# Layer 2's two blocks of a four-layer decoder: where the norms of batch 0 and batch 1 are made

## The reference, cut to what matters

```python
x = x + _L1_attn_ref(_layernorm(x, axis=-1), ...)
...
def _mha(x, y, ...):
    xn = _ln(x, lnx_g, lnx_b)
    yn = _ln(y, lny_g, lny_b)
    ...                       # 16 heads of 32, softmax of all scores, in block 1 masked after it
    x_out = x + o @ li1_w + li1_b
    h = jax.nn.gelu(_ln(x_out, ln3_g, ln3_b) @ li2_w + li2_b, approximate=False)
    return x_out + h @ li3_w + li3_b
x = _ln(xx, ln1_g, ln1_b)
x = x + _mha(x, x, ..., causal=True)
x = _ln(x, ln2_g, ln2_b)
return x + _mha(x, ee, ..., causal=False)
```

## Time and profile before

| | us |
|---|---|
| median of 3 runs | 2310.19 (2309.71 to 2314.41) |
| the profiled execution, its own time | 2309.87 |
| its span, first to last instruction | 2308.1 |

### The profile page before, as it was taken

One profiled execution on the slowest core, in us unless ns is written; L12 is line 12 of the kernel. 1 busy time (PEld: TensorE's weight loads), 2 busy tenths in 40 slices (PEclk: granted clock), 3 DMA queues, 4 the chain that ended last, 5 costly groups with the idle time before them and its releaser, 6 DMA issues.

```text
span 2308.1 us, 57670 instructions
## 1 busy us (share of the span) xinstructions
PE 2019.8 (88%) x22720; PEld 1471.6 (64%) x22720; DVE 1353.8 (59%) x3602; ACT 896.5 (39%) x3421; POOL 561.4 (24%) x1358
## 2 busy tenths in 40 slices
PE   8999999989977898998977887999999999789744
PEld 4899998877566565567855654666554545556522
DVE  6667666755255787545635624787263220678797
ACT  2455554543155564212334422665110111256511
POOL 3566664222011000102425512331000000401111
PEclk9555555999989899899988988999999999889956
DMA  3000002004000001100030000000030000000000
GB/s 136 4 5 5 5 5 79 1 1 182 0 5 2 14 12 53 86 0 24 1 133 2 1 1 7 9 11 2 1 151 0 1 0 4 1 15 12 2 0 16
DMA packets 8027, 57.21 MB, mean 25 GB/s; under 512 B 793, under 2 KB 5249, under 8 KB 5985
## 3 DMA queue, kind: packets, MB, share of 16 engines
q1 hardware_dynamic: 7760, 53.54, 6.1%
HBM read 52.62 MB, written 0.92 MB: 23 GB/s over the span
## 4 chain that ended last, share of the span: by engine, by line
PE 67%; DVE 12%; issue 9%; ACT 6%; POOL 5%; DMA 1%; POOLq 0%; DVEq 0%; SPq 0%; ACTq 0%
PE banks L265 43%; PE banks L270 8%; PE banks L1364 7%; PE banks L937 3%; ACT memory L985 2%; PE banks L963 2%; DVE memory L1466 2%; PE banks L1517 1%; DVE memory L1247 1%; ACT memory L1391 1%; DVE memory L824 1%; POOL memory L1423 1%; ACT memory L1398 1%; DVE memory L1472 1%; DVE memory L1475 1%
## 5 line engine op out<-in xcount | busy, mean ns | idle before, releaser
L265 PE MATMUL banks<-memory 128*112 128x256 f32 (+7 forms) x4192 | 1129.8, 425 | 65.9 <-POOL memory L2077 8.0
L265 PEld LDWEIGHTS banks<-memory 128*128 128x128 f32 (+3 forms) x4192 | 704.8, 195 | 396.4 <-issue 250.9
L270 PE MATMUL banks<-memory 112*125 112x112 f32 (+3 forms) x2000 | 305.9, 286 | 108.6 <-DVE memory L824 54.9
L270 PEld LDWEIGHTS banks<-memory 112*125 112x125 f32 (+3 forms) x2000 | 238.6, 172 | 224.6 <-issue 114.6
L1364 PE MATMUL banks<-memory 128*128 128x8 bf16 (+2 forms) x10752 | 308.1, 174 | 13.7 <-DVE memory L1449 1.4
L1364 PEld LDWEIGHTS banks<-memory 128*128 128x128 bf16 x10752 | 296.7, 104 | 25.7 <-POOL memory L1423 21.5
L985 ACT ACTIVATE memory<-banks,memory 112x375 f32<-112x375 f32 x384 | 215.4, 579 | 25.5 <-DVE memory L1023 25.1
L1023 DVE TENSOR_REDUCE memory<-banks 112x2 f32<-112x750 f32 x192 | 171.1, 934 | 37.1 <-PE banks L937 36.9
L1466 DVE TENSOR_REDUCE memory<-banks 128x48 f32<-128x192 f32 x448 | 122.1, 291 | 62.6 <-PE banks L1364 47.9
L840 POOL TENSOR_TENSOR memory<-memory 112x1 f32<-112x1 f32 x71 | 39.2, 552 | 355.7 <-DVE memory L819 354.3
L1031 DVE COPY memory<-banks 125x448 f32<-125x448 f32 x192 | 117.0, 620 | 10.5 <-PE banks L270 6.1
(11 more groups left out here) (234 smaller groups left out, 2425.2 us busy)
## 6 DMA issues: line engine op xcount, KB each, us to landing
memory<-in_l2x SPq DMA_DIRECT2D x1, 7680.0 KB, 21.6
memory<-in_l2f SPq DMA_DIRECT2D x1, 7168.0 KB, 20.1
memory<-in_l1f SPq DMA_DIRECT2D x1, 4617.0 KB, 14.8
memory<-in_ctxT SPq DMA_DIRECT2D x24, 187.5 KB
memory<-in_l2f SPq DMA_DIRECT2D x1, 4096.0 KB, 12.6
memory<-in_l3f SPq DMA_DIRECT2D x1, 3073.0 KB, 22.4
memory<-in_l2a SPq DMA_DIRECT2D x1, 3072.0 KB, 18.2
memory<-in_l0f SPq DMA_DIRECT2D x1, 2304.0 KB, 9.1
```

The costliest lines, as they stand in the source:

```text
L265: ins = self.nc.tensor.matmul(out, weights[i], acts[i], start=i == 0, stop=i == n - 1)
L270: return self.nc.tensor.transpose(out, in_, self.ident[0:n, 0:n])
```

## The change

Three things. First, batch 0's two norms of each block are made in the stage before the block: in layer 2's attention for block 1, by a new step `ahead` at the end of rounds 6, 7, 10 and 11 (statistics; then power, row, gain and shift on GpSimd; statistics of that; then power and row), and in the feed-forward between the blocks for block 2, with VectorE's parts after the adds of batch 3 and of batch 5. The base lies in `k.ahead`, the normalised row in a new buffer `k.ahead2`; the row is now made by GpSimd, which used to be VectorE's. The blocks' `prologue` loses `ln`, `stats` and `xn` of batch 0, and of `xm` only the copy with the bias stays. Second, in block 1 both norms of batch 1 go from `second` into `prologue`: statistics of the first ahead of everything, `xm` before the key projection, the second norm behind the query. Third, in layer 1's attention the statistics and the norm of batch 1 go from `second` into `prologue` too. In block 2 batch 1's norms stay in `second`. No DMA is added, moved or removed.

```diff
+        self.ahead2 = whole.take(D, parts=S)
...
+def ahead_block_dve(k, src, second):
+
+    if second:
+        k.nc.vector.wait_ge(*k.s.ahead_ready(1))
+    norm_row_stats(k, 0, k.ahead_stats, k.s.ahead_stat, k.ahead if second else src)
+
+
+def ahead_block_pool(k, src, rows, ln):
+
+    s, G = k.s, k.nc.gpsimd
+    norm_row(k, 0, k.ahead_stats, s.ahead_stat(1), s.ahead_rstd, k.ahead, src).then_inc(*s.gstep.up())
+    for n, op in ((ln, ALU.mult), (ln + 1, ALU.add)):
+        G.wait_ge(*s.gstep.now())
+        ins = G.tensor_tensor(k.ahead, k.ahead, rows[0:S, n, :], op)
+        ins.then_inc(*(s.gstep.up() if n == ln else s.ahead_ready.up()))
+
+
+def ahead_block_rows(k):
+
+    norm_row(k, 0, k.ahead_stats, k.s.ahead_stat(2), k.s.ahead_rstd, k.ahead2, k.ahead).then_inc(*k.s.ahead_ready.up())
...
-                xn = k.ahead if b < self.ahead else self.xn
+                xn = self.xn if b >= self.ahead else k.ahead2 if isinstance(self, L2Block) else k.ahead
...
-    prologue = (("xT", 0), ("parity", 0), ("k", 0), ("q", 0))
-    second = (("v", 0, 0), ("stats", 0, 1), ("xn", 0, 1), ("xT", 0, 1))
+    prologue = (("xT", 0), ("parity", 0), ("stats", 0, 1), ("k", 0), ("q", 0), ("xn", 0, 1))
+    second = (("v", 0, 0), ("xT", 0, 1))
...
+            if n in (6, 7, 10, 11):
+                yield "ahead", 0, (6, 7, 10, 11).index(n)
...
+        elif step == "ahead":
+            if i == 0:
+                V.wait_ge(*s.y_read(1))
+                ahead_block_dve(k, k.x[:, 0, :], False)
+            elif i == 2:
+                ahead_block_dve(k, k.x[:, 0, :], True)
...
-        if step == "stats":
+        if step == "ahead" and i == 3:
+            ahead_block_rows(k)
+        elif step == "ahead" and i == 1:
+            G.wait_ge(*k.landed["l2x_rows"].now())
+            G.wait_ge(*s.xT_full(1))
+            ahead_block_pool(k, k.x[:, 0, :], k.packs["l2x_rows"]["rows"], 0)
...
+    ahead = 1
...
-        return self.xms[b % 3]
+        return self.xms[b % 3] if b else self.k.ahead
...
-        elif step == "xm":
+        elif step == "xm" and b:
...
-            G.wait_ge(*s.xl_ready(b + 1))
-            G.tensor_tensor(xm, xm, self.row(self.ln), ALU.mult).then_inc(*s.gstep.up())
-            G.wait_ge(*s.gstep.now())
-            G.tensor_tensor(xm, xm, self.row(self.ln + 1), ALU.add).then_inc(*s.xm_ready.up())
-            G.wait_ge(*s.xm_ready(b + 1))
+            if b:
+                G.wait_ge(*s.xl_ready(b))
+                G.tensor_tensor(xm, xm, self.row(self.ln), ALU.mult).then_inc(*s.gstep.up())
+                G.wait_ge(*s.gstep.now())
+                G.tensor_tensor(xm, xm, self.row(self.ln + 1), ALU.add).then_inc(*s.xm_ready.up())
+                G.wait_ge(*s.xm_ready(b))
...
-    prologue = (("ln", 0), ("xm", 0), ("stats", 0), ("xn", 0), ("xT", 0), ("k", 0), ("q", 0))
-    second = (("v", 0, 0), ("ln", 0, 1), ("xm", 0, 1), ("stats", 0, 1), ("xn", 0, 1), ("xT", 0, 1))
+    prologue = (("ln", 0, 1), ("xT", 0), ("xm", 0), ("xm", 0, 1), ("k", 0), ("q", 0), ("stats", 0, 1), ("xn", 0, 1))
+    second = (("v", 0, 0), ("xT", 0, 1))
...
-    prologue = (("ln", 0), ("xm", 0), ("cstat", 0), ("stats", 0), ("cn", 0), ("xn", 0), ("xT", 0), ("q", 0), ("cT", 0),
-                ("k", 0), ("k", 1))
+    prologue = (("cstat", 0), ("cn", 0), ("xm", 0), ("xT", 0), ("q", 0), ("cT", 0), ("k", 0), ("k", 1))
...
+        else:
+            ahead_block_pool(self.k, self.into[:, 0, :], self.k.packs["l2x_rows"]["rows"], 2)
+            ahead_block_rows(self.k)
...
+            if not self.last and b in (HALF - 1, HALF + 1):
+                V.wait_ge(*s.x_ready(1))
+                ahead_block_dve(k, self.into[:, 0, :], b > HALF)
```

More of the change, by code:

```diff
@@ L1149, in order @@
     def order(self):
-        for kind, i in self.prologue:
-            yield kind, 0, i
+        for kind, i, *of in self.prologue:
+            yield kind, of[0] if of else 0, i
         yield "all", 0, 0
@@ L3221, in four_bit_rows, with norm_row_stats @@
         "p (i k n) -> p i k n", i=2, k=KD)
-def norm_row_stats(k, b, st, signal):
+def norm_row_stats(k, b, st, signal, src=None):
     s, V = k.s, k.nc.vector
-    V.bn_stats(st[:, 0:6], k.x[:, b, :]).then_inc(*s.vstep.up())
+    V.bn_stats(st[:, 0:6], k.x[:, b, :] if src is None else src).then_inc(*s.vstep.up())
     V.wait_ge(*s.vstep.now())
@@ L3232, in norm_row_stats, with norm_row @@
     V.tensor_scalar(st[:, 8:9], st[:, 7:8], EPS, None, ALU.add).then_inc(*signal.up())
-def norm_row(k, b, st, after, signal, into=None):
+def norm_row(k, b, st, after, signal, into=None, src=None):
     G = k.nc.gpsimd
@@ L3241, in norm_row @@
     into = k.row_norms[:, b, :] if into is None else into
[L3242 removed]
+    return G.tensor_scalar(into, k.x[:, b, :] if src is None else src, st[:, 6:7], st[:, 9:10], ALU.subtract, ALU.mult)
 def four_bit_values(k, values, y, sc):
```

2 lines of the change are left out of this document (1 added, 1 removed).

## The result

| | before | after |
|---|---|---|
| median of the runs compared, us | 2310.01 (2309.71 to 2314.41) | 2288.05 (2284.37 to 2290.48) |
| the profiled execution, its own time | 2309.87 | 2285.73 |
| its span | 2308.1 | 2283.9 |

The account below looks back on a forecast made before the run. TensorE, busy 88% of the span, was held to lose time only where it stands waiting for row norms or runs at half clock. Gains 3.1 + 12.6 + 5.0 = 20.7 us gave 2289.5 us, range 2283.5 to 2297.

Parts of the forecast that it names:

- Block 1, first wait: Block 1's head: without batch 0's norms on the path, the first row maximum comes 6.0 or 4.6 us earlier.
- Block 1, second wait: Batch 1's norm in block 1: its wait goes, ScalarE's value copy is late next, key projection gains 7.1 us.
- The rival, that another wait takes its place at the old time: Block 1: masks or exponentials hold TensorE's queue, the 7.1 us don't come; 13.6 instead of 20.7 us, 2296.6; chance 0.10.
- its counter-argument: Block 1: a mask is wanted only by its own four heads' transposes, said to stand behind the key projection.
- Block 1 together: Both waits of block 1 summed: 13.1 or 11.7 us gained, 12.6 taken.
- Layer 1's attention: Batch 1's norm wait goes, ScalarE's biased key copy is late next: neighbour matmuls 3.1 us earlier, between 1.8 and 3.53.
- Block 2: Block 2's head without batch 0's statistics and norms: query projection 5.3 us earlier; 5.0 us taken, between 3.8 and 6.5.
- up to 1.5 us are given back: Block 2's key matmuls: if the clock is still low there, up to 1.5 us of the gain is lost.
- What is added: Added statistics and norm steps in layer 2's attention and the feed-forward lie in idle time: nothing, bounds 0 and 1 us.
- The rival that ends slower than before: Late round of layer 2's attention: VectorE's wait for GpSimd's row delays the last output adds; 2315 if 26 us late; chance 0.02.
- The two clock cases: Clock low at all three heads and the keys: 2292.9, chance 0.13; clock stays high: 2283.7, chance 0.08.
- the prediction's slow case: Block 1's head: the 32 projections run mostly at half clock as before and take 5.38 us, against 4.1 at full.

Follow-up runs that it names:

- norm earlier: Changed kernel with batch 1's second norm in block 1 placed on VectorE ahead of the query instead of behind it; 2287.18 us, 0.9903 of before.
- both edits: Changed kernel with VectorE copying batch 0's values in block 1 and batch 1's second norm ahead of the query; 2282.14 us, 0.9872 of before.
- after, third: The changed kernel itself, unaltered, measured and profiled a third time; 2287.37 us, 0.9895 of before.
- Batch 0 only: Kernel before, with only batch 0's norms for block 1 made ahead in layer 2's attention; 2301.64 us, 0.9964 of before.
- value by VectorE: Changed kernel with batch 0's values in block 1 copied by VectorE instead of ScalarE; 2285.9 us, 0.9893 of before.

## Why the prediction held

**Block 1, first wait.** Right in its order, and in its bounds to 0.7 us. Projections were to start 2.6 us after the last add (1193.4 against 1190.84) and started 2.40 after it; they were to take 4.1 or 5.4 us and took 3.83 or 5.45; the maximum was to gain 6.0 or 4.6 and gained 6.7 (8.62 against 15.30) or 5.05. What was mis-sized: 0.16 us at the start of the projections, 0.27 in their full length, and batch 1's second norm ahead of the maximum, put at 0.8 us. It costs 0.56: "norm earlier" gives just that back at full clock (8.62 to 8.06), and "both edits" against "after, third" does at the slow one (10.25 to 9.69). "Batch 0 only", which has neither of batch 1's norms there, had its maximum 0.95 us earlier than the changed kernel at full clock; the other 0.39 are the first statistics ahead of the scaling (projections at 2.01 instead of 2.40).

**Block 1, second wait.** 7.1 us forecast, 7.04 measured (13.80 to 6.76), with the cause named beforehand and shown by "value by VectorE", which takes it away. The distance stood at 6.75 to 6.78 us in five profiles whatever the clock did. The rival, that another wait takes its place at the old time, is refuted by that. But its counter-argument was wrong in one step: the transposes that want the first mask stand ahead of the key projection, not behind it, and do wait for the mask (1.75 us, until 1197.76). It costs nothing because ScalarE's copy, at 1201.16, ends later still. The new wait of 2.94 us is the one that was forecast.

**Block 1 together.** 12.6 forecast; 11.1, 13.3 and 11.3 in three profiles, mean 11.9. The spread is the clock's, as the two bounds 11.7 and 13.1 had it, and slightly wider, because the loop behind adds its own. The assumption that an earlier head shifts all of its stage holds to 1.1 us here: the three profiles are 12.1, 13.7 and 12.1 us ahead at batch 1's key projection and 11.0, 13.3 and 11.3 at the block's end.

**Layer 1's attention.** 3.1 us forecast at the neighbour matmuls, 3.22 measured (15.05 to 11.83), bound by ScalarE's biased key copy as forecast. The statistics and the norm in the prologue cost the first maximum nothing. The whole layer gained 3.8 us on the mean of three profiles (411.02 to 407.23). In the first profile the attention's loop gave most of the gain back (107.70 us for the whole stage, before 108.65), and the unchanged stages behind it were 3.95 us shorter than before; in the other two the attention took 103.85 and 105.08, and the stages behind it were as long as before, to 0.3 us. The prediction had no term for such an exchange.

**Block 2.** 5.0 us taken, between 3.8 and 6.5; measured 6.5, 3.4 and 6.6 against the kernel before, 5.2 on the mean against 214.83. The query projection's gain was 6.16 us instead of 5.3: VectorE opened the stage 0.30 us after its release instead of 0.65, and the last of the context statistics, 0.48 us before, took 0.17; these two are 0.66 of the 0.86 us. The key matmuls at 1.53 or 2.87 us are the term "up to 1.5 us are given back". With the scores it is 2.2 us, so that the gain at the first maximum is 6.3 or 4.1 us, and over the whole block 6.5 or 3.4, the latter 0.4 below the forecast's bound.

**What is added.** Nothing, forecast and measured. The rival that ends slower than before needed GpSimd's row over 20 us after the last output adds; it was ready 25.7 us before VectorE came to wait for it.

**The clock.** The two clock cases were given 0.21 together as if one kernel had one answer for all its heads. The runs show each head falling its own way in each execution, so the mean is what a median of few runs finds, and both extreme cases are less likely than a mixture. The Trainium skill's "TensorE: Matmul & The Clock Gate", in "HAM oscillation — how this bites in real kernels", says that waits between short groups of matmuls put the array back to half rate so that each group starts slow. The trace agrees with the start of a group where the wait is long: after 2.94 us the key projection began at half rate in four of five profiles and took 3.54 or 3.73 us, and in "after, third" the clock fell 0.4 us after its start (3.34 us). It agrees at block 2's head too, where after 1.67 or 1.68 us the query projection began at half rate in every profile without unread matmuls. At block 1's head it doesn't: after 1.89 us the projections started at full rate in all three profiles of the changed kernel, and in two of them the clock fell while they ran. So the prediction's slow case came out right in length (5.4 forecast, 5.45 measured) partly by luck: it took the fall to lie in the pause, as before, and it lay inside the projections, which ran at half rate for about as long. Under "What's actually happening" the same page of the Trainium skill says that the count of slow matmuls at a kernel's start differs from run to run; these rows show the same in the middle of a kernel.

**The sum.** 3.1 + 12.6 + 5.0 = 20.7. By stages, means of three profiles of the changed kernel against those that leave a stage alone: 3.8 + 11.9 + 5.2 = 20.9, and 1.3 in layer 2's attention (139.03 to 137.69), which two of the three profiles have and the third has not, nor the kernel with the added work alone. That the stages with a forecast add up to within 0.2 us is luck in part, for layer 1 gave 0.7 more than its term and block 1 0.7 less; and the prediction had layer 2's attention as long as before, so the 1.3 there, which go with the clock, were not foreseen. The first profile's 24.2 us had the clock in its favour in layer 1, in layer 2's attention and in block 2.

## What to carry to other kernels

Where a tensor engine waits at a stage's head for a chain of small steps that cross two engines, look whether its input is ready in the stage before and whether the engines are idle there; then ask for each removed wait what comes next, and keep the measured distance to it. In block 1 the distance from the first maximum to batch 1's key projection was 13.8 us in all profiles with the old wait, and 6.75 to 6.78 in the five with the new one. When parts are compared, compare stages inside the traces, from an anchor right ahead of the edit: the time of a whole execution carries the clock's luck in stages that nobody touched, and the parts' medians added up to 26.4 us where the whole gave 18.8 to 24.1.

## What the runs showed of the hardware

- The same program in the same place has two lengths. Thirty-two matmuls behind a pause of 1.89 us took 3.83 or 5.45 us, and the keys of block 2 took 1.53 or 2.87. The lengths are repeated to 0.02 us; nothing lies between them at these places. Behind the drain and a wait of 1.39 or 1.40 us, in the kernels with block 1's old order, the thirty-two took 5.35 to 5.38 us in four profiles and 6.92 in one.
- A stage of layer 0 that no kernel changes took 131.4 to 131.5, 132.5 to 133.0, 134.4 to 134.9 or 136.5 to 136.7 us. Most of that arises in its first 40 us: the part to the fifth maximum took 37.2 us in the first profile of the changed kernel and 40.8 in that of both edits. This alone is more than the 0.2% that the prediction took for the measurement's limit.
- The granted clock can fall while TensorE is busy: in the first profile of the changed kernel it fell 1.6 us into block 1's 32 projections and stood at 0.50 for 3.3 us of them.
- Matmuls that nobody reads, in the pauses, did hold the granted clock at its upper level at three of three places, but they are as much in the way as useful ones when the pause is shorter than they are.
